# Seeding three transposed score groups a step from a bias tile in SBUF, with two-tensor forms for norms and maxima, in a one-core attention and mixture-of-experts kernel

## The reference

```python
x = x + attention(layernorm(x), ctx)        # 16 heads of 8 features
#   scores = Q K^T / sqrt(8) + m[h] * softplus(1000 + |i - j|); softmax over j; times V; Wo
h = layernorm(x)
shared = silu(h @ Sg) * (h @ Su) @ Sd
cw = top2(softmax(h @ Wr)) of 16 experts    # the two largest probabilities, 0 elsewhere
x = x + shared + sum_e cw[:, e] * (silu(h @ Wg[e]) * (h @ Wu[e])) @ Wd[e]
```

## Time and profile before

| | us |
|---|---|
| median of 3 runs | 248.23 (245.85 to 248.69) |
| the profiled execution | 247.91 |
| its span in the trace | 246.1 |
| TensorE busy | 222.8 (91%) |
| VectorE busy | 181.0 (74%) |
| ScalarE busy | 111.2 (45%) |
| GpSimd busy | 65.9 (27%) |

### The profile page before, as it was taken

One profiled execution on the slowest core, in us unless ns is written; L12 is line 12 of the kernel. 1 busy time (PEld: TensorE's weight loads), 2 busy tenths in 40 slices (PEclk: granted clock), 3 DMA queues, 4 the chain that ended last, 5 costly groups with the idle time before them and its releaser, 6 DMA issues.

```text
span 246.1 us, 6073 instructions
## 1 busy us (share of the span) xinstructions
PE 222.8 (91%) x1979; PEld 180.0 (73%) x1979; DVE 181.0 (74%) x644; ACT 111.2 (45%) x260; POOL 65.9 (27%) x119
## 2 busy tenths in 40 slices
PE   2886978899899998999899989999999889989995
PEld 2773556668698777877787869877887669768985
DVE  4699348965997589847996589658983899356882
ACT  8574445365325632464336432563256323752320
POOL 3500014010741047013811074105700380017000
PEclk9998699999999999999999999999999999999999
DMA  5651792425024510624051602460164300260000
GB/s 153 187 99 62 151 289 79 112 45 160 1 72 75 147 52 23 122 79 119 0 127 23 186 0 76 68 175 17 32 113 106 93 0 4 51 149 0 3 21 21
DMA packets 13078, 20.23 MB, mean 82 GB/s; under 512 B 2800, under 2 KB 9440, under 8 KB 12544
## 3 DMA queue, kind: packets, MB, share of 16 engines
q1 hardware_dynamic: 11856, 18.52, 31.1%
q10 hardware_dynamic: 1200, 1.43, 2.0%
HBM read 16.03 MB, written 3.78 MB: 81 GB/s over the span
## 4 chain that ended last, share of the span: by engine, by line
PE 44%; issue 30%; POOL 11%; DVE 8%; DMA 4%; ACT 1%; POOLq 0%; DVEq 0%; SPq 0%; ACTq 0%
PE ps_m L504 8%; PE ps_up L478 7%; POOL hid L1211 6%; PE ps_pv L413 4%; DVE nmax L881 4%; PE ps_st L384 4%; PE ps_st L394 4%; PE ps_up L483 3%; PE ps_pv L420 2%; POOL rstd L1183 2%; DMA stacks_sb<-qk_dram 2%; PE ps_up L292 2%; PE ps_st L446 1%; DMA ident<-in_c_ident 1%; DVE tg L987 1%
## 5 line engine op out<-in xcount | busy, mean ns | idle before, releaser
L987 DVE SCALAR_TENSOR_TENSOR tg<-th,ps_up 128x256 f32<-128x256 f32 x72 | 29.8, 414 | 29.3 <-ACT th L713 29.3
L668 ACT ACTIVATE probs<-ps_st 128x512 f32<-128x512 f32 x64 | 38.1, 598 | 25.1 <-PE ps_st L394 20.3
L713 ACT ACTIVATE th<-ps_up 128x256 f32<-128x256 f32 x72 | 27.6, 384 | 42.1 <-PE ps_up L483 42.0
L504 PE MATMUL ps_m<-wd_sb,hid 128*128 128x128 f32 x288 | 44.1, 280 | 0.6 <-DVE x_all L914 0.6
L881 DVE TENSOR_REDUCE nmax<-ps_s 128x4 f32<-128x512 f32 x64 | 42.6, 680 | 0.5 <-issue 0.4
L504 PEld LDWEIGHTS ps_m<-wd_sb,hid 128*128 128x128 f32 x288 | 37.6, 191 | 1.4 <-DVE x_all L914 1.0
L1211 POOL TENSOR_TENSOR hid<-hid,crep 128x512 f32<-128x512 f32 x28 | 35.1, 1274 | 3.8 <-DVE x2n L933 3.8
L993 DVE TENSOR_TENSOR hid<-tg,ps_up 128x256 f32<-128x256 f32 x72 | 29.8, 413 | 1.0
L478 PE MATMUL ps_up<-x_hi,wg_hi 128*128 128x256 f32 x72 | 26.6, 369 | 2.6 <-DVE hid L993 2.5
L351 PE MATMUL ps_s<-stacks_sb 96*128 96x128 f16 x256 | 23.8, 220 | 3.0 <-DVE nmax L881 2.5
L1179 POOL TENSOR_TENSOR ve<-mv,eps_sb 128x1 f32<-128x1 f32 x16 | 3.1, 192 | 84.7 <-DVE mv L926 84.7
(11 more groups left out here) (133 smaller groups left out, 442.3 us busy)
## 6 DMA issues: line engine op xcount, KB each, us to landing
crep<-cw_dram SPq DMA_DIRECT2D x28, 256.0 KB, 4.4
stacks_sb<-qk_dram SPq DMA_DIRECT2D x32, 128.0 KB, 3.7
qk_dram<-qk_parts SPq DMA_DIRECT2D x16, 128.0 KB, 1.8
out_y<-x_all SPq DMA_DIRECT2D x8, 128.0 KB, 4.0
wg_sb<-in_wgT ACTq DMA_DIRECT2D x1, 576.0 KB, 3.4
wu_sb<-in_wuT ACTq DMA_DIRECT2D x1, 576.0 KB, 3.4
wd_sb<-in_wd SPq DMA_DIRECT2D x1, 576.0 KB, 3.9
x_all<-in_x SPq DMA_DIRECT2D x2, 256.0 KB, 4.2
```

What stands on the lines that cost most here:

```text
L504: last = mm(ps_dn[:, b * P:(b + 1) * P], hid[:, buf, c, b * P:(b + 1) * P], wd_sb[:, c, :], start=(c == 0 and b == 0), stop=(c == SHARED), ...
L668: fn(probs[:, b, g * HG * P:(g + 1) * HG * P], ps_st[g % 2][:], ACT.Exp).then_inc(exp_sb, 1)
L713: fn(th[:, c % 2, :], ps_up[c % 2][:, 0, :], ACT.Tanh, scale=0.5).then_inc(tanh_sb, 1)
L987: v.scalar_tensor_tensor(out=tg[:, c % 2, :], in0=th[:, c % 2, :], scalar=1.0, in1=ps_up[c % 2][:, 0, :], op0=ALU.add, op1=ALU.mult).then_ ...
```

## The change

1. `bias_tiles` on TensorE computes the bias of the groups 0 and 1 once, ahead of the first step, into `ps_up[0]` and `ps_m`; `bias_copy` on VectorE brings both to a new tile `bias_T` in SBUF.
2. Three of the eight transposed score groups of a step are seeded: their bank gets the bias by a copy from `bias_T`, and the four score matmuls add to it. (b=0, g=0) is seeded by ScalarE (`seed_first`, after tanh 2, or after the shift rows in the first step), (1, 0) and (1, 1) by VectorE (`seed`, between hidden 4 and gate 5). The other five, (0, 1) among them, keep their bias matmuls.
3. The banks change places: group g uses `ps_st[(g + 1) % 2]`. So (0, 0) waits for `qklo_sb` and (0, 1) for `lsh_sb`. The projection of k no longer starts a group of its own in its bank.
4. `norm1` and `norm2` become scalar_tensor_tensor with the inverse deviation as a broadcast tensor; `max_high` becomes an add of zero.
5. The routing weights go to DRAM by SyncE's queue, just ahead of the reads.
6. Fillers: 24 and 2 in place of 36 ahead of the first step, and 28 in place of 6 in it.

```diff
+    bias_T = sb("bias_T", [P, 2, HG * P])
+    ps_bias = (ps_up[0][:].rearrange("p k t -> p (k t)"), ps_m[:])
...
     def spread_weights(f):
+        sp.wait_ge(cwT_sb, f + 1)
+        sp.dma_start(cw_dram[f], cwT[:]).then_inc(s_cwd, 16)
         sp.wait_ge(s_cwd, 16 * f + 16)
...
-    mm(ps_k0 if at_start(p) else ps_qk[:, T:2 * T], wT[:, 1, :], ctx_all[:, bass.ds(p * T, T)], start=True,
-       stop=True).then_inc(k_mm, 1)
+    mm(ps_k0 if at_start(p) else ps_qk[:, T:2 * T], wT[:, 1, :], ctx_all[:, bass.ds(p * T, T)],
+       start=at_start(p), stop=True, skip_group_check=True).then_inc(k_mm, 1)
...
+    def bias_tiles():
+        pe.wait_ge(s_dist, 16)
+        pe.wait_ge(act_setup, 2)
+        for g in range(2):
+            _, last = bias(ps_bias[g], g)      # the matmuls that stood in scores_T
+            last.then_inc(bias_mm, 1)
...
-    def scores_T(a, b, g, buf, f=None, p=None):
-        bank = ps_st[g % 2]
+    def scores_T(a, b, g, buf, f=None):
+        bank, n, seeded = ps_st[(g + 1) % 2], 2 * NHG * a + NHG * b + g, (b, g) in ((0, 0), (1, 0), (1, 1))
         if f is not None:
             pe.wait_ge(lsh_sb, f + 1)
-        if p is not None:
-            pe.wait_ge(qklo_sb, 2 * p + 2)
-        if at_start(a) and b == 0:
-            if g >= 2:
-                pe.wait_ge(exp_sb, g - 1)
-        else:
-            pe.wait_ge(exp_sb, 2 * NHG * a + NHG * b + g - 1)
+        if (b, g) == (0, 0):
+            pe.wait_ge(seed0_sb, a + 1)
+        elif seeded:
+            pe.wait_ge(seed1_sb, 2 * a + g + 1)
+        elif not (at_start(a) and b == 0 and g < 2):
+            pe.wait_ge(exp_sb, n - 1)
...
+        first = False if seeded else bias(bank, g)[0]
...
+    def seed_first(a, p):                      # ScalarE
+        if p is not None:
+            act.wait_ge(qklo_sb, 2 * p + 2)
+        if at_start(a):
+            act.wait_ge(bias_sb, 2)
+        fn(ps_st[1][:], bias_T[:, 0, :], ACT.Copy).then_inc(seed0_sb, 1)
...
-    def weights_out(f):
-        act.wait_ge(cwT_sb, f + 1)
-        act.dma_start(cw_dram[f], cwT[:]).then_inc(s_cwd, 16)
...
-    last = v.tensor_scalar(xn[:, b, :], x_all[:, p * NB + b, :], mv1[:, b, 0:1], rstd1[:, b:b + 1],
-                           ALU.subtract, ALU.mult)
+    last = v.scalar_tensor_tensor(out=xn[:, b, :], in0=x_all[:, p * NB + b, :], scalar=mv1[:, b, 0:1],
+                                  in1=rstd1[:, b:b + 1].to_broadcast([P, P]), op0=ALU.subtract, op1=ALU.mult)
...
-    v.tensor_copy(nsplit[:, b, 0, :], nmax[:, b, :]).then_inc(nh_sb, 1)
+    v.tensor_tensor(nsplit[:, b, 0, :], nmax[:, b, :], zero[:].to_broadcast([P, H]), ALU.add).then_inc(nh_sb, 1)
...
+    def bias_copy(g):                          # VectorE, ahead of the first step
+        dve.wait_ge(bias_mm, g + 1)
+        v.tensor_copy(bias_T[:, g, :], ps_bias[g]).then_inc(bias_sb, 1)
+
+    def seed(a, g):                            # VectorE
+        dve.wait_ge(exp_sb, 2 * NHG * a + NHG + g - 1)
+        v.tensor_copy(ps_st[(g + 1) % 2][:], bias_T[:, g, :]).then_inc(seed1_sb, 1)
...
     hidden(f, 4, 1 - abuf)
+if as_:
+    seed(a, 0)
+    seed(a, 1)
+if fs:
     gate(f, 5)
...
     v.memset(stacks_sb[:, 1].bitcast(F32), 0.0).then_inc(dve_pads, 1)
+    bias_copy(0)
+    bias_copy(1)
+    dve.wait_ge(bias_sb, 2)
     v.memset(select[:], 0.0)
```

More of the change, by code:

```diff
@@ L305, in project_q @@
                     pe.wait_ge(s_wqkvo, 32)
-                mm(ps_qk[:, 0:T], wT[:, 0, :], xnT[:], start=True, stop=True).then_inc(q_mm, 1)
+                mm(ps_qk[:, 0:T], wT[:, 0, :], xnT[:], start=True, stop=True, skip_group_check=True).then_inc(q_mm, 1)
             def project_k(p):
@@ L360, in shift_T, with bias @@
                 nc.tensor.transpose(ps_nm, nsplit[:, b, :, :].rearrange("p s h -> p (s h)"), ident16[:]).then_inc(nm_mm, 1)
-            def scores_T(a, b, g, buf, f=None, p=None):
-                bank = ps_st[g % 2]
+            def bias(bank, g):
+                h0, first, last = HG * g, True, None
+                n_split = min(max(SPLIT_SLOPES - h0, 0), HG)
+                n_small = min(max(SPLIT_SLOPES + SMALL_SLOPES - h0, 0), HG) - n_split
+                if n_split:
+                    for part in (slope_hi, slope_lo):
+                        last = mm(bank[:, 0:n_split * P], dist16[:], part[:, h0:h0 + n_split, :], start=first, stop=False,
+                                  skip_group_check=True)
+                        first = False
+                if n_small:
+                    j = h0 + n_split - SPLIT_SLOPES
+                    last = mm(bank[:, n_split * P:(n_split + n_small) * P], dist16[:], slope_small[:, j:j + n_small, :],
+                              start=first, stop=False, skip_group_check=True)
+                    first = False
+                return first, last
+            def bias_tiles():
[6 more added lines that the diff above has]
+                bank, n, seeded = ps_st[(g + 1) % 2], 2 * NHG * a + NHG * b + g, (b, g) in ((0, 0), (1, 0), (1, 1))
                 if f is not None:
                     pe.wait_ge(lsh_sb, f + 1)
-                if p is not None:
-                    pe.wait_ge(qklo_sb, 2 * p + 2)
-                if at_start(a) and b == 0:
-                    if g >= 2:
-                        pe.wait_ge(exp_sb, g - 1)
-                else:
-                    pe.wait_ge(exp_sb, 2 * NHG * a + NHG * b + g - 1)
+                if (b, g) == (0, 0):
[4 more added lines that the diff above has]
+                    pe.wait_ge(exp_sb, n - 1)
                 if g == 0:
@@ L378, in scores_T @@
                         pe.wait_ge(act_pads, 2)
[L379 to L393, removed]
+                first = False if seeded else bias(bank, g)[0]
+                for h in range(HG * g, HG * g + HG):
+                    o = (h - HG * g) * P
                     last = mm(bank[:, o:o + P], ks[buf][:, h, b * P:(b + 1) * P], qs[buf][:, h, b * P:(b + 1) * P],
@@ L423, in attention_T @@
             def attention_T(a, b, f):
+                if at_start(a) and b == 0:
+                    pe.wait_ge(bias_sb, 2)
                 pe.wait_ge(attn_sb, 2 * a + b + 1)
@@ L516, in step @@
                 if as_: scores(a, 0, 1, abuf)
+                if not fs: keep_clock(1)
                 if ps:
@@ L521, in step @@
                 if as_: scores(a, 0, 2, abuf)
+                if not fs: keep_clock(3)
                 late_down(1)
@@ L524, in step @@
                 if as_: scores(a, 0, 3, abuf)
+                if not fs: keep_clock(2)
                 if fs: up(f, 0)
@@ L587, in _ @@
             project_x(1)
-            keep_clock(36)
+            keep_clock(24)
+            bias_tiles()
+            keep_clock(2)
             step(None, 0, 1, 2, 0)
@@ L667, in exponential @@
                     act.wait_ge(pv_mm, 2 * a + b - 1)
-                fn(probs[:, b, g * HG * P:(g + 1) * HG * P], ps_st[g % 2][:], ACT.Exp).then_inc(exp_sb, 1)
+                fn(probs[:, b, g * HG * P:(g + 1) * HG * P], ps_st[(g + 1) % 2][:], ACT.Exp).then_inc(exp_sb, 1)
+            def seed_first(a, p):
[4 more added lines that the diff above has]
+                fn(ps_st[1][:], bias_T[:, 0, :], ACT.Copy).then_inc(seed0_sb, 1)
             def shift_rows(a, b, buf):
@@ L731, in step @@
                     tanh(f, 2)
+                if as_ and fs: seed_first(a, p)
+                if fs:
                     router_exp(f)
@@ L737, in step @@
                     shift_rows(a, 1, abuf)
-                    if not fs: exponential(a, 0, 0)
+                    if not fs:
+                        seed_first(a, p)
+                        exponential(a, 0, 0)
                     exponential(a, 0, 1)
@@ L932, in norm2 @@
                     dve.wait_ge(x2T_mm, a)
-                v.tensor_scalar(x2n[:, b, :], x1_all[:, a * NB + b, :], mv2[:, b, 0:1], rstd2[:, b:b + 1],
-                                ALU.subtract, ALU.mult).then_inc(x2n_sb, 1)
+                v.scalar_tensor_tensor(out=x2n[:, b, :], in0=x1_all[:, a * NB + b, :], scalar=mv2[:, b, 0:1],
+                                       in1=rstd2[:, b:b + 1].to_broadcast([P, P]), op0=ALU.subtract,
+                                       op1=ALU.mult).then_inc(x2n_sb, 1)
             def x2_low(f):
```

11 lines of the change are left out of this document (7 added, 4 removed).

## The result

The changed kernel takes 246.58 us (median of 6 runs, 246.03 to 250.93), the kernel before 248.16 in the same session. The ratio is 0.994, with a 95% interval of 0.991 to 0.997: 1.6 us faster by the medians, where 9.9 were forecast. The forecast was 238.2 us, and the measured time lies above its range of 234.6 to 244.8. The one execution at 250.93 us had a lower mean TensorE clock (0.973) than the others, and the ratio leaves it out.

A forecast was written before the change was run, and what follows sets the result against it. Bound by a chain of waits through VectorE, then TensorE, then VectorE and GpSimd. Terms 1.2 + 4.2 + 2.6 + 1.9 + 0 + 0 = 9.9 us off 247.91 gave 238.0, as median 238.2; range 234.6 to 244.8.

The forecast's parts named there:

- the cast: Cast of the maxima as an add of zero on VectorE: not held, 0.17 us; 0.2 us in six steps, 1.2 us.
- the norms: x2n of b=0 at step end: 0.35 us instead of 1.27, residual 0.6 us earlier, seven times, 4.2 us; norm 1 nothing.
- The port rival: GpSimd holds VectorE instructions with two SBUF inputs just as the old forms; 5.4 us go, 243.6 us; chance 0.20.
- Bias of (0,0): Two 512-column bias matmuls leave TensorE's chain, ScalarE's copy being covered: 0.43 us in six steps, 2.6 us.
- Bias of (1,0): Bias matmuls replaced by a VectorE copy; TensorE waits 0.15 us, gain 0.28 in seven steps, 1.9 us.
- the late-seed rival: A copy into PSUM costs 1.3 us instead of 0.65; TensorE waits 0.8 us at (1,0), 242.7 us; chance 0.13.
- Bias of (1,1): Bias matmuls before values_T only fill TensorE's wait for ScalarE's copy of ps_pv; removing them gains 0.
- Routing DMA as cover: Move to SyncE starts ScalarE's exponential of (0,3) some 0.6 us earlier; own gain 0, left in place 0.3 us a step lost.
- First step: Two bias copies on VectorE lose 1.3 us; removed matmuls and a held-up clock regain 1.3; sum 0.
- The clock rival: New small waits let TensorE's granted clock fall within the steady steps: slower than before, 257 us; chance 0.07.

The follow-up runs named there:

- the first experiment: The changed kernel with norm 1, norm 2 and the cast of the maxima in their old forms (tensor_scalar, tensor_copy): 246.07 us, ratio 0.992 to the kernel before.
- the reduction: The changed kernel with the cast of the maxima as a tensor_reduce over one element: 244.05 us, ratio 0.985 to the kernel before.
- the earlier product: The changed kernel with GpSimd's product of pair 0 ahead of both inverse deviations: 241.86 us, ratio 0.977 to the kernel before.
- both reliefs: The changed kernel with the maxima cast as a one-element reduction and GpSimd's product of pair 0 ahead of both inverse deviations: 239.84 us, ratio 0.965.

## Why the prediction was wrong

**The steps that failed are the cast and the norms.** "It is not held. So I take 0.17 for the new form" rested on one kind of row: L891, two SBUF inputs, 0.17 us beside L1193. L1193 is two short adds of 128x128, and in the kernel before L891 always came after the product had ended. It never met the instruction that the new forms meet. As soon as an edit moved it forward by a microsecond or more, it took 0.35 to 0.56 us. Even against the adds the row proves nothing. L891 ends at 96.28, and the first add, alone in GpSimd's timeline of the kernel before, ends at 96.25:

```profile
95.79 0.46 POOL L1193 TENSOR_TENSOR xb<-x_all,bo_rep 128x128 f32<-128x128 f32 x1
```

The low half ends 0.03 to 0.04 us after the first add in all six steps, in the kernel before and in the change alike. That is the distance at which the held instructions end behind the product. So it may have run between the two adds, and "six times of six" is one and the same arrangement, repeated. The port rival, with a chance of 0.20, was the truth about these two terms: 5.4 us forecast, and a small loss measured (x2n 1.34 to 1.36 us instead of 1.27 to 1.29; 0.6 us in the six full steps, by the first experiment). The rule of the Trainium skill (SBUF — State Buffer, Who interferes with whom) agrees with what the product does to every VectorE instruction with two SBUF inputs here: the add (0.81 to 1.01 us instead of 0.17), x2n and L926. By the same rule L926 should wait for the adds, which read SBUF; no row here decides that, for the reason just given. The old forms, with one tensor and a scalar or none, are held by the product as well (the first experiment); the reduction isn't.

**The sum of both terms was right in size.** Other means to the same end gave 5.0 us in the kernel before, 5.4 forecast. In the change the earlier product gave 4.7 us (norms, 4.2 forecast). The reduction gave 2.5 us there, twice the 1.2 forecast for the cast; it also frees what the seed of (0,0) had saved, so the cast's own share isn't known. The limit that I set the norms, TensorE's L433, was what came next.

**Bias of (0,0), 2.6 us: failed for a second reason.** I took it as independent of the cast. It isn't: with the cast still held, VectorE reaches the second half of the maxima late, and the 0.43 us that TensorE saves ahead of it turn into a wait of 0.46 at 101.78. That reading rests on the timelines; no run takes this seed out of the change itself. I had even written that VectorE's 0.6 us would be used up there, and then gave the rival that takes them away only the 5.4 us of its own terms. That is most of why the port rival stood at 243.6 and the kernel at 246.6. With both reliefs the seed gives 1.2 us. There too a wait follows, up to 0.24 us a step, put down to the exponential of (0,0).

**Bias of (1,0), 1.9 us: within what was measured**, which is wide: 1.3 to 2.9 us. The seed by VectorE takes 686 ns (0.65 taken), ScalarE's 598 (0.60 taken), so the late-seed rival falls. **Bias of (1,1), 0: right**; leaving it out changes 0.2 us, within the spread. With this seed TensorE waits 0.39 us for the copy of ps_pv, and without it not at all. The edit is work without a return.

**Routing DMA as cover, 0: right in sense.** Taken back, 1.0 to 1.2 us are lost; I said 0.3 us a step. **First step, 0 from 1.3 lost and 1.3 regained: the sum was right.** The change's first marked x2n is 0.15 us later; the fillers win 1.4 us of it and the rest loses 1.5. That the two bias copies are what loses it isn't shown. They hold the first row maximum back to 18.74 us, but with the copies on ScalarE the first mark came only 0.4 us earlier. **The clock rival** fell for the six full steps: 1.00 in all profiles. In the step before them the clock did fall again, for some 3.4 us, in four profiles whose first step had lost it too (the change with the old forms and three versions with both edits), but not in the change's own.

Put together: cast and norms a little under 0, (0,0) near 0, (1,0) 1.3 or more, first step 0. From the first mark to the last the change is 2.0 us shorter, up to it 0.15 longer, and the medians differ by 1.6. The split between the two seeds within the change is argued, not measured.

## What to carry to other kernels

An instruction that isn't held in a trace proves something only if it met the instruction that is said to hold it. List both engines' intervals and look for the pair, before an edit is costed on it. When a rival takes a term away, follow what else leaned on that term: a late VectorE also eats what was saved on TensorE ahead of it. Where one engine holds another, moving one of them in time (4.7 us here) was the surest. Another form of the same instruction helped only where it doesn't meet the hold at all: of the forms tried, the reduction alone ran through (2.5 us).

## What was not expected of the hardware

- A reduction over one element with one SBUF input (128x16) ran in 0.17 us beside GpSimd's product of 128x512, where a copy took up to 1.01 and an add of two tensors up to 1.01. Instructions with one of two tensors in PSUM run through as well: L1032 takes 0.42 us at 94.43 beside the product, in the trace of the reduction. Whether L926 is held by GpSimd's adds of 128x128 stays open.
- TensorE's granted clock fell to 0.50 behind short idle stretches in the first step (24.7 to 26.0 and 28.1 to 29.0 us in the version with both edits), in some executions and not in others. It stayed there for some 10 us and fell once more for some 3.4 us in the second step; such executions are 4.6 us longer. With thirteen more filler transposes (7 and 6) none of 24 executions shows it (mean clock 0.993 or more, against 0.972 with it).
- The write of the routing weights took 1.43 to 1.60 us until SyncE went on, in nearly all steps, and 2.1 to 3.5 in a few.
